# Graph network layer on one core: three of thirteen sorted blocks stay unsorted, their rows gathered by POOL, and a float32 scatter of the sorted messages

## The reference

```
e   = edge_attr @ edge_W[k] + edge_b[k]          # 53125 x 128
msg = relu(x[src] + e)                           # gather of node rows
agg = segment_sum(msg, dst)                      # scatter onto nodes
z   = (1 + eps[k]) * x + agg
h   = relu(batchnorm(z @ W1[k] + b1[k]))
x   = relu(layernorm(h @ W2[k] + b2[k]) * ln_g + ln_b)
```

## Time and profile before

| | |
|---|---|
| Median of 3 runs (range) | 1601.37 us (1601.23 to 1604.98) |
| Profiled execution, its own time | 1590.61 us |
| Its span, first to last instruction | 1588.7 us |
| Mean granted TensorE clock | 0.857 |
| PE busy | 1185.8 us, 75% |
| PEld (weight loads, beside PE) | 997.2 us, 63% |
| DVE busy | 924.6 us, 58% |
| ACT busy | 548.6 us, 35% |
| POOL busy | 864.1 us, 54% |
| DMA | 309.89 MB, mean 195 GB/s |

### The profile page before, as it was taken

The page is one execution under the profiler, slowest core; times in us unless marked ns, Lnnn a source line. Parts: engine busy times, 40 slices in busy tenths (PEclk is TensorE's granted clock), DMA queues, the critical chain, the costliest instruction groups (busy, mean ns, idle before and its releaser), DMA issues.

```text
span 1588.7 us, 33542 instructions
## 1 busy us (share of the span) xinstructions
PE 1185.8 (75%) x12492; PEld 997.2 (63%) x12492; DVE 924.6 (58%) x1858; ACT 548.6 (35%) x1146; POOL 864.1 (54%) x842
## 2 busy tenths in 40 slices
PE   4665676667798788886588877878957878878786
PEld 2333333356687677775477777767846767767685
DVE  7575456566676666666354455445663546555557
ACT  1232223233444444442233333333422333333333
POOL 6777677756555545532664555554256545554550
PEclk8788778787988989987698998998967989999988
DMA  9998999985665556666355555555645555655552
GB/s 240 314 346 299 325 339 341 340 287 163 202 186 171 172 166 192 184 177 194 90 177 147 163 164 148 169 140 170 186 111 146 177 154 153 177 153 169 165 140 60
DMA packets 252731, 309.89 MB, mean 195 GB/s; under 512 B 53005, under 2 KB 169791, under 8 KB 252583
## 3 DMA queue, kind: packets, MB, share of 16 engines
q1 hardware_dynamic: 208734, 218.79, 45.2%
q0 software_dynamic: 33280, 82.06, 16.7%
q10 hardware_dynamic: 10569, 6.97, 1.8%
HBM read 200.17 MB, written 107.55 MB: 194 GB/s over the span
## 4 chain that ended last, share of the span: by engine, by line
PE 63%; issue 20%; DVE 9%; DMA 4%; another core or an unknown queue 2%; ACT 1%; SPq 1%; DVEq 0%; ACTq 0%
PE ps L1525 34%; PE ps L1552 10%; PE ps L1542 9%; PE ps L1506 5%; DMA ep_dram<-terms 3%; DVE terms L1074 3%; PE ps L1576 2%; PE ps L1568 1%; PE ps L1561 1%; PE ps L1574 1%; DVE hot_stage L1092 1%; PE ps L1508 1%; DVE xr L950 0%; DVE early_words L1001 0%
## 5 line engine op out<-in xcount | busy, mean ns | idle before, releaser
L638 POOL DMA_INDIRECT rows<-table_dram,src_i x416 | 422.4, 1015 | 426.5 <-DVE terms L1177 237.3
L1170 DVE TENSOR_TENSOR terms<-ps,terms 128x512 f32<-128x512 f32 x156 | 107.7, 691 | 431.1 <-PE ps L1525 223.0
L1525 PE MATMUL ps<-xs,early_words 125*128 125x128 bf16 x2720 | 295.1, 232 | 70.2 <-issue 62.1
L1525 PE MATMUL ps<-xs,region 125*128 125x128 bf16 x2584 | 279.8, 232 | 65.9 <-issue 65.4
L638 POOL DMA_INDIRECT rows<-x_dram,src_i x208 | 214.5, 1031 | 170.6 <-DVE terms L1177 117.5
L1525 PE MATMUL ps<-xr,early_words 125*128 125x128 bf16 x1360 | 268.9, 232 | 28.3 <-issue 27.8
L1525 PEld LDWEIGHTS ps<-xs,early_words 125*128 125x128 fp8e4 x2720 | 234.4, 104 | 87.6 <-issue 79.5
L1506 PE MATMUL ps<-wf,attr_x 64*128 64x384 f32 x416 | 195.1, 622 | 105.7 <-issue 53.1
L658 POOL DMA_INDIRECT srt_dram<-region,pos_i x208 | 225.0, 1082 | 86.5 <-issue 61.4
L1525 PE MATMUL ps<-xr,region 125*128 125x128 bf16 x1292 | 255.6, 232 | 21.2 <-issue 20.8
L1525 PEld LDWEIGHTS ps<-xs,region 125*128 125x128 fp8e4 x2584 | 223.2, 104 | 74.8 <-issue 74.4
(11 more groups left out here) (135 smaller groups left out, 1860.9 us busy)
## 6 DMA issues: line engine op xcount, KB each, us to landing
ep_dram<-terms SPq DMA_DIRECT2D x52, 768.0 KB
terms<-srt_dram SPq DMA_DIRECT2D x156, 256.0 KB
terms<-ep_dram SPq DMA_DIRECT2D x156, 256.0 KB
early_words<-hotrow_dram SPq DMA_DIRECT2D x156, 104.0 KB
attr_x<-attr_dram SPq DMA_DIRECT2D x52, 256.0 KB
region<-kept_dram SPq DMA_DIRECT2D x13, 576.0 KB
early_words<-kept_dram SPq DMA_DIRECT2D x13, 576.0 KB
region<-kept_dram SPq DMA_DIRECT2D x13, 560.0 KB
```

Of the source, the lines that this page charges most:

```text
L638: pool.indirect_dma_start(rows[:, q, t * FEAT:(t + 1) * FEAT], None, source, bass.IndirectOffsetOnAxis(ap=src_i[:, c:c + 1], axis=0),).the ...
L1170: nc.vector.tensor_tensor(terms[:, q, :], bank(q), terms[:, q, :], ALU.add).then_inc(s_added, 1)
L1525: ins = nc.tensor.matmul(bank(q)[:, c:c + FEAT], hot_g[v % 2][0:SLICE, h, at:at + P], x_part(part, FIRST[t] + k), start=k == 0 and part == ...
```

## The change

Bodies 3, 7 and 11 are named UNSORTED. Their first block is not sorted any more:

- In staging, VectorE copies and adds its e (`staged_rows`), and SP stores the rows in order, with four DMAs a quad, where ScalarE and POOL's indirect DMAs did it.
- In the layers, TensorE skips `gather` for these bodies. POOL gathers their 16 x 128 rows with indirect DMAs as well (`gather_s`), into four buffers `rows_s`, one quad at a time, each behind a regular quad in one of the three bodies in front (SPREAD). For body 3 the places are behind quad 2 of body 0, quad 1 of body 1, and quads 0 and 3 of body 2. `add_s` takes the rows from there instead of PSUM.
- For all bodies, `parts` is gone: the sorted messages are scattered in float32, 16 matmuls of 144 columns with a float32 one-hot matrix, instead of 48 in bfloat16.
- VectorE's loop in the second layer is written out. Counting of the semaphores is adapted. The one-hot matrices of the three bodies are still made, stored and loaded.

```diff
+UNSORTED = (3, 7, 11)
+SPREAD = {(body - BLOCK_QUADS + at // BLOCK_QUADS, at % BLOCK_QUADS): (body, n) for body in UNSORTED
+          for n, at in enumerate((6, 9, 12, 15))}
...
-        hot_s = sb("hot_s", [P, 2, QUAD * SORT_WINDOW], bf16)
+        hot_s = sb("hot_s", [P, 2, QUAD * SORT_WINDOW])
...
-        rest_s = attr_x[:, 0:2, :]
+        rows_s = [attr_x[:, n, :] for n in range(ATTR_SLOTS)] + [later[:, 0:QUAD * FEAT]]
...
+            def store_unsorted(j, q):
+
+                es_out(sp, j * BLOCK_QUADS + q, 1)
+                for t in range(QUAD):
+                    at = j * BLOCK_EDGES + (q * QUAD + t) * P
+                    sp.dma_start(srt[at:at + P, :], stage_s[:, q, t, :]).then_inc(stored_plain[q], 16)
...
+                if j in UNSORTED:
+                    store_unsorted(j, q)
                 sp.wait_ge(ep_taken, half_of(n + 1, 1))
...
+            def gather_s(l, source, j, q):
+
+                at = UNSORTED.index(j)
+                if at >= 1:
+                    pool.wait_ge(s_added, quad_at(l, UNSORTED[at - 1], q) + BLOCK_QUADS + 1)
+                elif l >= 1:
+                    pool.wait_ge(s_added, quad_at(l - 1, UNSORTED[-1], q) + BLOCK_QUADS + 1)
+                elif q == 0:
+                    pool.wait_ge(ep_taken, half_of(LAYER_QUADS, 1))
+                    es_out(pool, LAYER_QUADS - 1, 1)
+                for t in range(QUAD):
+                    c = 2 * j * BLOCK_TILES + q * QUAD + t
+                    pool.indirect_dma_start(
+                        rows_s[q][:, t * FEAT:(t + 1) * FEAT], None, source,
+                        bass.IndirectOffsetOnAxis(ap=src_i[:, c:c + 1], axis=0),
+                    ).then_inc(gathered_s[q], 16)
...
-                    for q in range(BLOCK_QUADS):
+                    for q in range(0 if j in UNSORTED else BLOCK_QUADS):
...
+                            if (j, q) in SPREAD:
+                                gather_s(l, source, *SPREAD[j, q])
...
+            def staged_rows(n):
+
+                j, q = divmod(n, BLOCK_QUADS)
+                shape = [P, 2, LAYERS, FEAT]
+                c = j * BLOCK_TILES + q * QUAD
+                rows_stored(dve, q, j)
+                nc.vector.tensor_copy(stage_s[:, q, :, LAYERS * FEAT:LAYERS * FEAT + 2], meta_u[:, c:c + QUAD, :])
+                for half in range(2):
+                    tiles = slice(2 * half, 2 * half + 2)
+                    dve.wait_ge(es_filled, half_of(n, half))
+                    nc.vector.tensor_tensor(
...
+                        eb_all[:, :, :].unsqueeze(1).to_broadcast(shape), ALU.add).then_inc(es_kept, 1)
...
-                nc.vector.tensor_tensor(terms[:, q, :], bank(q), terms[:, q, :], ALU.add).then_inc(s_added, 1)
+                of = rows_s[q] if j in UNSORTED else bank(q)
+                nc.vector.tensor_tensor(terms[:, q, :], of, terms[:, q, :], ALU.add).then_inc(s_added, 1)
...
-                nc.vector.tensor_tensor(left, whole, high(whole, n), ALU.subtract).then_inc(s_rest, 1)
-                dve.wait_ge(s_rest, at + 1)
-                nc.vector.tensor_tensor(last, left, high(left, n), ALU.subtract).then_inc(s_parts, 1)
...
+                if j in UNSORTED:
+                    return
...
                 for t in range(QUAD):
-                    for part in (high(whole, QUAD * FEAT), high(left, QUAD * FEAT), high(last, QUAD * FEAT)):
-                        ins = nc.tensor.matmul(ps[:, bass.ds(col, SORT_WINDOW)], part[:, t * FEAT:(t + 1) * FEAT],
+                    ins = nc.tensor.matmul(ps[:, bass.ds(col, SORT_WINDOW)], terms[:, q, t * FEAT:(t + 1) * FEAT],
```

More of the change, by code:

```diff
@@ L72, in node, with served @@
     return l * NODE_TILES + t + 1
+def served(j):
+    return sum(body < j for body in UNSORTED)
 def pair_at(t, k):
@@ L216, in build @@
         later = early_words[:, hots_words + hot_words:]
-        last_s = later[:, 0:2 * QUAD * FEAT].rearrange("p (h e) -> p h e", h=2)
         def node_buffer(n):
@@ L304, in build @@
         es_taken = sem("es_taken")
+        es_kept = sem("es_kept")
         scattered = [sem(f"scattered{n}") for n in range(BLOCK_QUADS)]
+        stored_plain = [sem(f"stored_plain{n}") for n in range(BLOCK_QUADS)]
         ep_filled = sem("ep_filled")
@@ L321, in build @@
         gathered = [sem(f"gathered{n}") for n in range(BLOCK_QUADS)]
+        gathered_s = [sem(f"gathered_s{n}") for n in range(BLOCK_QUADS)]
         x_biased = sem("x_biased")
@@ L393, in groups, with quad_at, rows_stored, es_out @@
             return [slice(g * GROUP, min((g + 1) * GROUP, NODE_TILES)) for g in range(GROUPS)]
+        def quad_at(l, j, q):
+            return l * LAYER_QUADS + j * BLOCK_QUADS + q
+        def rows_stored(eng, q, bodies):
+            eng.wait_ge(scattered[q], (bodies - served(bodies)) * 16 * QUAD)
+            if served(bodies):
+                eng.wait_ge(stored_plain[q], served(bodies) * 16 * QUAD)
+        def es_out(eng, n, half):
+            j = n // BLOCK_QUADS
+            if n >= 0 and j in UNSORTED:
+                eng.wait_ge(es_kept, half_of(n - (j - served(j)) * BLOCK_QUADS, half))
+            elif n >= 0:
+                eng.wait_ge(es_taken, half_of(n - served(j) * BLOCK_QUADS, half))
         def half_of(n, half):
@@ L664, in _ @@
                         pool.wait_ge(table_ready, 16 * (NODE_TILES - EARLY_NODES) * l)
-                    for j in range(l == 0, BODIES):
+                    for j in range(BODIES):
                         for q in range(BLOCK_QUADS):
-                            pool.wait_ge(p_added, (l * BODIES + j) * BLOCK_QUADS + q - BLOCK_QUADS + 1)
-                            gather(l, source, j, q)
+                            if l + j >= 1:
+                                pool.wait_ge(p_added, (l * BODIES + j) * BLOCK_QUADS + q - BLOCK_QUADS + 1)
+                                gather(l, source, j, q)
+                            if (j, q) in SPREAD:
+                                gather_s(l, source, *SPREAD[j, q])
             with pool.Else():
@@ L926, in _ @@
             step(nc.vector.memset(ones_b[:, :], 1.0))
-            for semaphore, value in ((es_taken, 2), (ep_taken, 2), (ep_stored[0], 16), (ep_stored[1], 16),
+            for semaphore, value in ((ep_taken, 2), (ep_stored[0], 16), (ep_stored[1], 16),
                                      (g_filled, BLOCK_QUADS), (s_added, BLOCK_QUADS), (s_done, BLOCK_QUADS),
@@ L1253, in turn @@
                 def turn(q):
-                    parts(l, j, q)
                     if q < BLOCK_QUADS - 1:
@@ L1384, in _ @@
                     if l < LAYERS - 1:
-                        with dve.Fori(2, BODIES - 1) as j:
+                        for j in range(2, BODIES - 1):
                             body(l, j, True, True, False)
@@ L1501, in staged @@
                 for half in range(2):
-                    pe.wait_ge(es_taken, half_of(n, half))
+                    es_out(pe, n - 1, half)
                     pe.wait_ge(ep_taken, half_of(n, half))
```

41 lines of the change are left out of this document (21 added, 20 removed).

## The result

The changed kernel takes 1770.78 us, median of 4 runs (1767.31 to 1772.13), against 1601.3 us for the kernel before in the same comparison: ratio 1.1064, 95% interval 1.1027 to 1.1101. It is slower by 170 us. The forecast was 1697 us in a range to 1775: the direction is right, the size was 74 us short.

A forecast was written before the change was run, and what follows sets the result against it. The prediction took TensorE to bound the layers, starved during POOL's long indirect-DMA runs. Its terms, -94 + 155 + 30 + 0 + 5 = +96 us, moved the median from 1601.4 to 1697 us; own range 1630 to 1775, 8-in-10 range 1540 to 1775.

The forecast's parts named there:

- The reading of the bound: Layers: TensorE bounds them and starves while POOL issues indirect DMAs without a pause; 9 to 10 us of holes per body.
- The signs named: Profile after: issue above 20%, runs of eight or more, holes of 6 us, 36 us bodies, lower clock, records 0.12 to 0.13 us.
- The extra gathers: Layers: 36 extra quads on POOL lengthen its runs and cost TensorE 4.3 us each, +155 us (+65 to +230).
- the upper bound: Extra quads: all 5.2 us lost and the clock down behind, 6.4 us per quad, +230 us.
- The unsorted bodies: Nine layer bodies without 204 gather matmuls each shrink from 31.2 to 20.8 us, -94 us (-47 to -146).
- Both rows give about 21: Unsorted bodies: POOL's 16 row gathers (20.8 us) and a layer's last body (21.3 us) as grounds for -94.
- The float32 scatter: Sorted scatter, 32 records instead of 48: +1.0 us in 30 body visits, +30 us (+18 to +135).
- I put their going at nothing: VectorE's two dropped subtractions, 215 us of work: no effect on time; at most -54 us, no cost.
- Staging: 48 scatters leave POOL for plain SP stores, VectorE takes additions: +5 us, as the DMA engines set the pace.
- Fewer matmuls win: Rival, chance 0.28: TensorE's holes are its own, extra quads cost nothing while POOL is not the bound; -59, 1542 us.
- A short hole per extra quad: Rival, chance 0.12: extra quads find their own pauses and cost 1.8 us each; +6, 1607 us.
- Float32 loads in line: Rival, chance 0.05: float32 scatter weight loads are not hidden, +135 instead of +30 us; 1802 us.

The follow-up runs named there:

- experiment 1: Separate probe without the computation: 420 TensorE matmuls beside 20 instructions of another engine; 55 ns a matmul beside plain DMAs, only 109 in 25 us beside indirect ones.
- experiment 2: Changed kernel with no unsorted body, float32 scatter kept: 1587.11 us, ratio 0.9917 to the kernel before; again in another job 1581.65 us, ratio 0.9897.
- experiment 3: Kernel before plus the 36 extra quads of POOL gathers into a buffer nobody reads: 1802.51 us, ratio 1.1283; again in another job 1798.08 us, ratio 1.1233.
- experiment 7: Whole change, unaltered, in a job where the kernel before took 1230.01 us: 1397.87 us, ratio 1.1342; the unaltered matmul probe there passed 413 matmuls beside indirect DMAs.

## Why the prediction was right, and where not

**The reading of the bound: shown.** TensorE's missing time beside POOL's runs was the ground of the whole forecast, and experiment 1 has it with nothing else in the way. The signs named came out: "issue" 24% (above 20%), runs of twelve, holes of 9 us (6 and more), bodies with extra quads of 35.2 and 37.5 us (36), clock 0.770 (lower than 0.857), scatter records at 0.12 us (0.12 to 0.13), first layer at 352.6 us (before 370). One did not: the unsorted bodies were to take 20 to 22 us, and in the second layer theirs are 37.9, 37.8 and 33.3 us.

**The extra gathers: right mechanism, undersized.** 200 to 204 us in three comparisons against 155: 5.6 us per quad, more than the 5.2 us that POOL works on one. The term was 0.83 of 5.2 us, the loss at full clock; the upper bound, in which all 5.2 us are lost and the clock falls behind it (6.4 us), was nearer. The granted clock of the layers (0.75 against 0.87) says that the clock's part was no side matter.

**The unsorted bodies: the step that failed.** -94 was taken and -47 was its weak end; -18 was measured, staging included, some -24 in the layers. "Both rows give about 21", the step said, and a stretch of 18.2 us does stand there. But it counted POOL's 16 DMAs as a floor of the short body alone. POOL's DMAs that the short body doesn't hold come in a run of twelve in the next, and in a long run TensorE passes next to nothing, be its stream of 300 matmuls or of 130. The pair must be counted, not the body: 54.8 us for two against 60 in experiment 2 (twice its mean), not 21 + 30.

**The float32 scatter: priced right for itself, wrong in its sum.** +30 was taken with nothing for VectorE; the record spacing was as forecast, and both edits together gave -12 to -17. That lies between the ends named (+18 less 54), so "I put their going at nothing" is the part that fell. Of the Trainium skill's rule ("TensorE: Matmul & The Clock Gate", Weight-path perf modes) that FP32 weights don't get the fast load, the trace bears out what was drawn from it: eight plain-scatter records stand 0.105 us apart and 144 columns don't double that.

**Staging:** +7 for +5, which says little: in experiment 3, where staging is that of the kernel before, the first layer began at 339.6 us in one execution and at 349.1 in the other.

In sum: -18 instead of -89 for the bodies with staging, +202 instead of +155, and -12 instead of +30. Two misses of about 71 and 47 us on the low side, and one of 42 the other way. That 1770.8 lies inside the range, 4 us under its upper end, is luck as far as the size goes: had the float32 scatter cost its +30, the same change would have come out above 1800. The direction and the cause were not luck.

**The rivals.** "Fewer matmuls win" is out in the job of the result: experiment 3 adds nothing to TensorE's stream and costs 200 us. The Trainium skill's rule behind it ("SBUF — State Buffer", Who interferes with whom), that TensorE never waits on anyone, speaks of ports of the on-chip memory. Whether a port is at work here no run shows; taken as the prediction took it, as a rule on time, it fails in experiment 1 (109 matmuls where 413 fit) and holds for the same probe in experiment 7. The rule of the Trainium skill's "Runtime: NRT & Kernel Launch" (Instruction fetch mechanics), that fetching is mostly hidden, is not contradicted by the holes, as the prediction had it: in those of experiment 1 no transfer of the instruction queue is under way. Even where the rule holds its conclusion failed, since the limit that the rival itself named, "as long as POOL is not the bound", was reached: I set it against bodies of 31.2 us, and without holes a body of the kernel before takes some 23 us (1230 less 345 of staging, over 39 bodies, an estimate) while five quads need 26. "A short hole per extra quad", 1.8 us each, is out, since 5.6 us each were measured. Float32 loads in line are out by the spacing.

**What stays open.** Which part of the chip TensorE and POOL's indirect DMAs share is not shown; it is not memory traffic as such. The number of matmuls ahead of the first hole (68 and 88) suggests a store that runs out or one that fills up. That it is TensorE's instruction supply is not borne out by the instruction queue, and would not by itself make the signals of VectorE and ScalarE late. One rival nobody tested: that the recording of the traces is what gets held up beside POOL's indirect DMAs, and holds up the engines in turn. It would fit the late and missing events, and every run on record has a recorded span and clock, so none shows the kernel without it. Also open are how long a run may be, and what makes a job one with holes. The same number of chip stood over a job at 1231 and later over one at 1598 us, so it is either a condition that changes, or the number does not name one piece of silicon.

## What to carry to other kernels

Before work is moved from a busy engine to one that looks half idle, look at what the idle engine's instructions do to the others while they run: 144 more indirect DMAs, whose rows nobody uses, cost 200 us in jobs with holes; and where there are none, the changed kernel was 168 us slower because, by its chain, POOL was full. Look also whether the kernel takes the same time in another job, and compare within one. Then count by pairs of stages, because an engine that works ahead pays back behind a shortened stage what it could not do in it. And split a change of several edits: the one thought to cost 30 us, the float32 scatter, alone made the kernel 1% faster in two jobs with holes (in one without it was not run).

## What the runs showed of the hardware that was not expected

- 20 indirect gathers of 128 rows by POOL, 1.25 us apart, cut TensorE's rate from 55 ns to some 600 ns a matmul (some 40 in the 24.4 us from 31.4 to 55.8), in holes near multiples of 0.7 us; 20 plain DMAs or memsets of POOL did nothing.
- In two of the jobs the probe and the changed kernel had none of this: the kernel before took 1230 us instead of 1600, and 20 gathers beside TensorE left it at 413 matmuls in 25 us.
- The holes begin 68 matmuls of 128 columns (3.8 us) or 88 of 384 columns (14.3 us) after POOL's run does, and no 16 KB transfer of the instruction queue is under way in the first kind (none from 31.5 to 61.9 us).
- In jobs with holes the semaphore events of TensorE, VectorE and ScalarE come over 1 us late or are missing (346 of 865, 333 of 1,330, 479 of 1,685 in the changed kernel; 3, 6 and 12 in a job without), none of TensorE's where POOL had begun no indirect DMA for 8 us. One wait of VectorE for a matmul that ended at 1077.4 us was over at 1088.5.
- A wait of POOL for the landing of a quad's gathers costs 3.4 us in the mean.
